# A gated cross-attention and quantised FFN layer: unrolled program, tiles batch by batch, int8 quantisation by conversion, 80 columns a head

## The reference

```
n  = layernorm(x)
q, k, v = n @ Wq, ctx @ Wk, ctx @ Wv            # per head 64 columns, 77 keys
x  = x + tanh(g_xattn) * (softmax(q k' / 8) v @ Wo + bo)
fq(t, f) = clip(round(t * 2**f), -128, 127) / 2**f
h  = relu(fq(fq(layernorm(x), 4) @ fq(w1, 6)' + fq(b1, 6), 4))    # 1024 hidden
x  = x + tanh(g_ffn) * (fq(h, 4) @ fq(w2, 6)' + fq(b2, 6))
```

## Time and profile before

| | |
|---|---|
| median of 3 executions | 143.04 us (142.93 to 143.25) |
| profiled execution: span | 141.0 us (no other time is given for it) |
| busy: PE / weight load | 133.5 us (95%) / 115.7 us (82%) |
| busy: DVE / ACT / POOL | 114.3 (81%) / 86.4 (61%) / 71.7 us (51%) |
| chain that ended last | PE 72%, DVE 14%, DMA 4%, issue 3%, ACT 3% |
| granted TensorE clock | 1.000 of full speed throughout |
| HBM read | 6.46 MB, nearly all in the first 21 us |

### The profile page before, as it was taken

One profiled execution on the slowest core, in us unless ns is written; L12 is line 12 of the kernel. 1 busy time (PEld: TensorE's weight loads), 2 busy tenths in 40 slices (PEclk: granted clock), 3 DMA queues, 4 the chain that ended last, 5 costly groups with the idle time before them and its releaser, 6 DMA issues.

```text
span 141.0 us, 3229 instructions
## 1 busy us (share of the span) xinstructions
PE 133.5 (95%) x1010; PEld 115.7 (82%) x1010; DVE 114.3 (81%) x282; ACT 86.4 (61%) x174; POOL 71.7 (51%) x104
## 2 busy tenths in 40 slices
PE   5959899999999999999999999999999999999991
PEld 2749898779998997989888898989898989768670
DVE  1077788998899999988987898889888889977572
ACT  3238174355877475894949495767757593828350
POOL 7522869989652753544555455544636364240200
PEclk9999999999999999999999999999999999999999
DMA  4999980000000000000020010002000200020204
GB/s 100 308 315 375 378 340 19 0 0 2 7 0 0 0 7 0 0 0 0 5 74 2 0 65 10 0 0 74 0 0 0 74 0 0 5 74 0 74 5 149
DMA packets 6295, 8.69 MB, mean 62 GB/s; under 512 B 489, under 2 KB 4237, under 8 KB 6285
## 3 DMA queue, kind: packets, MB, share of 16 engines
q1 hardware_dynamic: 6285, 8.56, 18.1%
HBM read 6.46 MB, written 2.10 MB: 61 GB/s over the span
## 4 chain that ended last, share of the span: by engine, by line
PE 72%; DVE 14%; DMA 4%; issue 3%; ACT 3%; POOL 1%; SPq 1%; DVEq 0%; ACTq 0%; POOLq 0%
PE sc_ps L840 17%; PE of_ps L912 16%; PE of_ps L953 7%; PE h_ps L944 6%; PE tr_ps L889 6%; DMA x_sb<-in_x_dram 4%; PE tr_ps L798 3%; PE tr_ps L868 2%; PE h_ps L868 2%; PE sc_ps L953 2%; PE of_ps L957 2%; DVE hid L659 2%; DVE den L594 2%; DVE mx L559 2%; PE tr_ps L777 1%
## 5 line engine op out<-in xcount | busy, mean ns | idle before, releaser
L912 PE MATMUL of_ps<-u_sb,pT 128*128 128x256 f32 x240 | 33.5, 288 | 0.0
L307 POOL TENSOR_TENSOR probs<-probs,rden 128x616 f32<-128x616 f32 x16 | 19.5, 1219 | 24.5 <-DVE rden L597 24.5
L840 PE MATMUL sc_ps<-a_sb,xT 128*128 128x308 f32 x192 | 31.3, 312 | 0.6 <-DVE a_sb L588 0.5
L912 PEld LDWEIGHTS of_ps<-u_sb,pT 128*128 128x128 f32 x240 | 29.7, 189 | 1.2 <-ACT pT L460 1.0
L840 PEld LDWEIGHTS sc_ps<-a_sb,xT 128*128 128x128 f32 x192 | 27.5, 188 | 1.4 <-DVE a_sb L588 0.7
L460 ACT CAST pT<-tr_ps 128x640 fp32r<-128x640 f32 x16 | 11.1, 692 | 23.2 <-PE tr_ps L889 23.2
L484 ACT ACTIVATE hid<-h_ps,b1z 128x256 f32 (+1 forms) x56 | 22.0, 480 | 0.5 <-PE h_ps L944 0.5
L314 POOL TENSOR_TENSOR rstd<-ve,mhalf 128x1 f32<-128x1 f32 x16 | 8.8, 553 | 21.4 <-DVE nm L631 21.4
L322 POOL TENSOR_TENSOR pT<-pT_full,pT 128x640 fp32r<-128x640 f32 x9 | 14.1, 1562 | 1.6 <-ACT pT_full L465 1.6
L944 PE MATMUL h_ps<-x2T,w1T 128*128 (+1 forms) x112 | 14.5, 273 | 0.0
L953 PE MATMUL of_ps<-w2T,hid 128*128 128x256 bf16 x104 | 13.6, 272 | 0.3 <-issue 0.3
(11 more groups left out here) (143 smaller groups left out, 221.4 us busy)
## 6 DMA issues: line engine op xcount, KB each, us to landing
x_sb<-in_x_dram SPq DMA_DIRECT2D x8, 256.0 KB, 7.2
w_sb<-in_L_ffn_w_dram SPq DMA_DIRECT2D x2, 1024.0 KB, 9.4
out_dram<-x_sb SPq DMA_DIRECT2D x7, 256.0 KB, 2.1
wk_sb<-in_L_xattn_Wk_dram SPq DMA_DIRECT2D x1, 512.0 KB, 3.8
wq_sb<-in_L_xattn_Wq_dram SPq DMA_DIRECT2D x1, 512.0 KB, 6.3
wv_sb<-in_L_xattn_Wv_dram SPq DMA_DIRECT2D x1, 512.0 KB, 9.8
wo_sb<-in_L_xattn_Wo_dram SPq DMA_DIRECT2D x1, 512.0 KB, 10.6
out_dram<-x_sb SPq DMA_DIRECT2D x2, 128.0 KB, 2.0
```

Of the source, the lines that this page charges most:

```text
L307: nc.gpsimd.tensor_tensor(v, v, rden[:, i, :].unsqueeze(2).to_broadcast([P, H, M]), ALU.mult).then_inc(probs_ready, 1)
L840: ins = nc.tensor.matmul(sc_ps[:, a, 0:HALF], xT[:, i, p, c, :], a_sb[:, q, c, i, HALF * a:HALF * a + HALF], start=first, stop=last)
L912: ins = nc.tensor.matmul(attn_ps, pT[:, i, p, P * c:P * c + P], u_sb[:, q, MC * i + c, :], start=first, stop=last)
```

## The change

The program is written anew with the same engines and the same arithmetic:

- **Order of tiles**: T = 8b + t, batch 0 first. Only batch 0's folded weights and U are made before slot 0; batch 1's are made in slots 0 to 3 (`score_weights(1, c)`, `output_weights(1, n)`), like w1's and w2's transposes. All slots are written out; there is no loop. x is looked ahead by 3 to 4 slots, scores by 2, hidden lags by 4, the second layer by 6.
- **80 columns a head**: probabilities have a pitch of 80 (3 padding columns). A chunk of U is then made of pieces of 32, 64 or 128 output rows at fixed places, ten a batch (`U_PIECES`), each one plain matmul with `tile_position`; bo is a matmul over 128 rows.
- **int8 by conversion**: writing to an int8 tile rounds and clamps. The second normalisation is one POOL instruction from x to int8; the hidden layer is a Relu on ACT to int8 (`hid_q`), widened to bf16 by POOL (`hidden_widen`, two copies of 512 columns); weights are rounded by ACT in one pass. Two int8 values are transposed as one bf16.
- **Engines**: the first normalisation moves from ACT to POOL; epsilon and the negated mean of the second from DVE to POOL; the low part of the probabilities is on POOL for tiles 0 to 3, on DVE for 4 to 15. Zeroing of kz and vz moves from POOL to DVE.
- **Second bias**: one bf16 row in a 128-row tile (`first_row`, `b2_row`), no offset, no DMA between tiles.
- **DMAs**: x comes in four pieces in the order of the batches, the first after wq; g comes broadcast to all rows.

The core of the diff:

```diff
-EARLY, LATE = 5, TILES - 2
+EARLY = 4
+U_PIECES = ((0, 0, 128, 0, 0),
+            (1, 0, 32, 0, 128), (1, 32, 32, 1, 0), (1, 64, 64, 1, 32),
+            (2, 0, 64, 1, 96), (2, 64, 64, 2, 0),
+            (3, 0, 64, 2, 64), (3, 64, 32, 2, 128), (3, 96, 32, 3, 0),
+            (4, 0, 128, 3, 32))
...
+            def output_weights(b, n):
+                for c, row, rows, j, col in U_PIECES:
+                    if c // 2 != n:
+                        continue
+                    dst = u_banks[b, n][:, D * (c % 2):D * (c % 2) + D]
+                    ins = nc.tensor.matmul(dst[row:row + rows, :], vz[:, b, j, col:col + rows], wo_sb[:, j, :],
+                                           start=True, stop=(c > 0), tile_position=(0, row))
+                    if c == 0:
+                        ins = nc.tensor.matmul(dst, bo_at[:, :], bo_pad[:, :], start=False, stop=True)
+                ins.then_inc(u_psum, 1)
...
+            # POOL
+            def normalise_first(T):
+                pool.wait_ge(rstd1_ready, T // 2 + 1)
+                if T >= 2:
+                    pool.wait_ge(xT_psum, T - 1)
+                nc.gpsimd.tensor_scalar(xn[:, T % 2, :], x_sb[:, T, :], rstd1[:, T:T + 1], nb1[:, T:T + 1],
+                                        ALU.mult, ALU.add).then_inc(xn_ready, 1)
+            def normalise_second(T):
+                i = T % 2
+                pool.wait_ge(mv2_ready, T + 1)
+                nc.gpsimd.tensor_scalar(ve2[:, i, :], mv2[:, i, 1:2], EPS, 1.0 / (AQ * AQ), ALU.add, ALU.mult).then_inc(ve2_ready, 1)
+                pool.wait_ge(ve2_ready, T + 1)
+                nc.gpsimd.tensor_tensor(rstd2[:, i, :], ve2[:, i, :], mhalf[:, 0:1], ALU.pow).then_inc(rstd2_ready, 1)
+                pool.wait_ge(rstd2_ready, T + 1)
+                nc.gpsimd.tensor_scalar(nb2[:, i, :], mv2[:, i, 0:1], rstd2[:, i, 0:1], -1.0, ALU.mult, ALU.mult).then_inc(nb2_ready, 1)
+                pool.wait_ge(nb2_ready, T + 1)
+                if T >= 2:
+                    pool.wait_ge(yT_psum, T - 1)
+                nc.gpsimd.tensor_scalar(yq[:, i, :], x_sb[:, T, :], rstd2[:, i, 0:1], nb2[:, i, 0:1],
+                                        ALU.mult, ALU.add).then_inc(yq_ready, 1)
+            def hidden_widen(k):
+                p, half = k // 2, k % 2
+                for n in range(2):
+                    if k == FC * 2 - 1 and n == 1:
+                        pool.wait_ge(hid_last, 1)
+                    else:
+                        pool.wait_ge(hid_rounded, 2 * k + n + 1)
+                    c = 4 * half + 2 * n
+                    nc.gpsimd.tensor_copy(hid[:, p, c:c + 2, :, :].rearrange("p c i r -> p (c i r)"),
+                                          hid_q[:, (2 * k + n) % 4, :]).then_inc(hid_ready, 1)
...
+            for s in range(TILES + 4):
+                if live(s - 1):
+                    normalise_second(s - 1)
+                if s == 0:
+                    rstd_first(3)
+                if s == 1:
+                    rstd_first(4)
+                if s < EARLY:
+                    probsT_low(s)
+                if live(s + 1):
+                    softmax_scale(s + 1)
+                if s == 2:
+                    hidden_bias()
+                    output_bias()
+                if s in (3, 4, 5):
+                    rstd_first(s + 2)
+                if 0 <= s - 4:
+                    hidden_widen(s - 4)
+                if live(s + 4):
+                    normalise_first(s + 4)
...
+            # ACT, hidden layer
+                for c in range(2):
+                    chunk = 4 * half + 2 * n + c
+                    ins = nc.scalar.activation(hid_q[:, (2 * k + n) % 4, D * c:D * c + D], h_ps[:, n, D * c:D * c + D],
+                                               ACT.Relu, bias=b1z[:, chunk:chunk + 1])
...
+            # DVE, one slot
+                if live(s - 1):
+                    residual(s - 1)
+                    stats_second(s - 1)
+                if live(s + 1):
+                    denominators(s + 1)
+                if s == 0:
+                    stats_first(3)
+                if s == 1:
+                    stats_first(4)
+                if s in (3, 4, 5):
+                    stats_first(s + 2)
+                if s >= EARLY:
+                    probsT_low(s)
+                if live(s + 3):
+                    rowsT_low(s + 3)
...
+                if live(s - 6):
+                    result(s - 6)
+                if live(s + 2):
+                    center(s + 2)
...
+            # PE, one slot
+            for s in range(TILES):
+                if live(s + 3):
+                    rowsT(s + 3)
+                if s == 0:
+                    pe.wait_ge(u_ready, 2)
+                    score_weights(1, 0)
+                probsT(s)
+                if s == 1:
+                    pe.wait_ge(a_ready, 3)
+                    score_weights(1, 1)
+                    weights1T()
+                if s == 2:
+                    pe.wait_ge(a_ready, 4)
+                    output_weights(1, 0)
+                    output_weights(1, 1)
+                if s == 3:
+                    pe.wait_ge(u_ready, 4)
+                    output_weights(1, 2)
+                    weights2T()
+                if s >= 4:
+                    hidden(s - 4)
+                if s >= 2:
+                    quantisedT(s - 2)
+                if s >= 6:
+                    ffn_out(s - 6)
+                if live(s + 2):
+                    scores(s + 2)
+                attend(s)
```

More of the change, by code:

```diff
@@ L11 @@
 F32R = mybir.dt.float32r
+I8 = mybir.dt.int8
 P = 128
@@ L148, in flamingo_kernel @@
[L148 to L159, removed]
+        attn_ps = of_ps[:, 0, 0:D]
@@ new lines, in rowsT_second, with round_weights @@
+            def rowsT_second(T):
+                act.wait_ge(yT_psum, T + 1)
+                nc.scalar.copy(x2T[:, T // 2, :, T % 2, :],
+                               yT_of(T).bitcast(I8).rearrange("p (r c) -> p c r", c=DK)).then_inc(x2T_ready, 1)
+            def round_weights(w_in, w_sb, w_q, done):
+                act.wait_ge(w_in, 16)
+                src, dst = w_sb[:, :, :].rearrange("p a b -> p (a b)"), w_q[:, :, :].rearrange("p a b -> p (a b)")
+                for h in range(2):
+                    nc.scalar.activation(dst[:, 1024 * h:1024 * h + 1024], src[:, 1024 * h:1024 * h + 1024], ACT.Copy,
+                                         scale=WQ).then_inc(done, 1)
@@ L517, in _ @@
[L517 to L529 removed]
+            a_copy(0, 0)
@@ new lines, in _ @@
+            residual(TILES - 1)
+            stats_second(TILES - 1)
+            for T in range(TILES - 6, TILES - 2):
+                result(T)
+            last = FC - 1
+            dve.wait_ge(hid_psum, 4 * TP)
+            dve.wait_ge(hid_ready, 4 * TP - 4)
+            for c in range(2):
+                chunk = FC - 2 + c
+                ins = nc.vector.tensor_scalar(hid_q[:, 3, D * c:D * c + D], h_ps[:, 1, D * c:D * c + D],
+                                              b1z[:, chunk:chunk + 1], 0.0, ALU.add, ALU.max)
@@ L749, in _ @@
+            ins.then_inc(hid_last, 1)
+            for T in range(TILES - 2, TILES):
+                result(T)
         @block.tensor
@@ new lines, in scores @@
+            def scores(T):
+                pe.wait_ge(xT_high, T + 1)
+                if T >= 1:
+                    pe.wait_ge(centered, T)
+                if T == TB:
+                    pe.wait_ge(a_ready, 2 * DK)
+                for p, q in PARTS:
+                    if p == 1:
+                        pe.wait_ge(xT_ready, T + 1)
+                    for c in range(DK):
+                        for a in range(2):
+                            first, last = (c, p, q) == (0, *PARTS[0]), (c, p, q) == (DK - 1, *PARTS[-1])
+                            ins = nc.tensor.matmul(sc_ps[:, a, 0:HALF], xT[:, T % 2, p, c, :],
+                                                   a_sb[:, q, T // TB, c, HALF * a:HALF * a + HALF], start=first, stop=last)
+                ins.then_inc(scores_ready, 1)
@@ new lines, in ffn_half, with ffn_bias, ffn_out @@
+            def ffn_half(T, half):
+                p, i = T // 2, T % 2
+                pe.wait_ge(hid_ready, 4 * p + 2 * half + 2)
+                for c in range(4 * half, 4 * half + 4):
+                    nc.tensor.matmul(ffn_of(T), hid[:, p, c, i, :], w2T[:, c, :], start=(c == 0), stop=False)
+            def ffn_bias(T):
+                nc.tensor.matmul(ffn_of(T), first_row[:, :], b2_row[:, :], start=False, stop=True).then_inc(ffn_psum, 1)
+            def ffn_out(T):
+                if T == 0:
+                    pe.wait_ge(w2T_ready, 2)
+                    pe.wait_ge(b2_ready, 1)
+                    pe.wait_ge(consts, 6)
+                elif T not in ffn_last:
+                    pe.wait_ge(result_ready, T)
+                ffn_half(T, 0)
+                ffn_half(T, 1)
+                ffn_bias(T)
```

1098 lines of the change are left out of this document (437 added, 661 removed).

## The result

The changed kernel takes 144.59 us (median of 4 executions, 144.03 to 145.75) against 143.10 for the one before: a ratio of 1.0101, 95% interval 1.0052 to 1.0151. It is slower, where 141.7 and faster were forecast. In what follows medians are over all executions of a kernel, while ratios leave out those more than 1.5% above its fastest. The profiled execution took 145.03 with a span of 143.1, so what lies around the span is 1.93 (2.04 was taken).

The account below looks back on a forecast made before the run. PE was taken to set the steady slots (6.7 to 6.2 us) and POOL the first six; slot 6 at 67.8, last attention at 125.8 and a 13.9 tail gave span 139.7, plus 2.04 made 141.7 us, range 137.6 to 147.

Parts of the forecast that it names:

- Steady slot: Repeating per-tile slot on PE: falls from 6.7 us to 6.2, range up to 6.5.
- The rival that the gaps stay: Steady slots: 0.2 us gaps stay without the loop, slots stay at 6.5 us, 143.7 us in all; chance 0.15.
- Slots 0 to 5: Early slots with batch 1's weights inside, scheduled from POOL's order: slot 0 at 23.1 us, slot 6 at 67.8.
- idle PE: Early slots: POOL costs the start about 6 us of PE standing idle.
- POOL's terms: POOL's work in a slot: 1.33 us to the statistics plus 4.5, 5.8 in all, against 6.2 on PE.
- the two-input price: Dearer end for POOL's new 256- and 512-column instructions: 1.98 ns a column, where one-input L344's price was taken.
- the slack: Steady slot: POOL's 5.8 us chain leaves 0.4 us against PE's 6.2.
- the second rival: POOL sets every slot: its chain 1.0 us longer, 7.2 us added, 148.9 us in all; chance 0.18.
- batch 1's output weights: Slot 2 on PE: ten matmuls taken at 4.7 us.
- the third rival: Output weight pieces overlap, start better than scheduled: 1.8 us less for each batch, 138.2 us in all; chance 0.22.
- Tail: After the last attention: 13.9 us with overlaps, against 12.2 before the change.
- The sign: Whole kernel: 141.7 us against a median of 143.04; faster 0.63, same 0.09, slower 0.28.

Follow-up runs that it names:

- the fill experiment: Changed kernel with ten more matmuls of 512 columns, result unused, inside attention(0) before its wait for the low part: 143.76 us, ratio 1.0044 against the kernel before.

## Why the prediction was wrong

The span is 3.4 us over the forecast. By stages, from the table above: slot 1 took 1.6 more than forecast, slot 3 1.1, slot 4 0.6, slot 5 0.1, the slots from 6 on 0.6 and the tail 0.6; slot 2 took 0.6 less, slot 0 0.2 less, and slot 0 began 0.4 early.

- **Steady slot, right.** 6.2 was worked out, 6.15 to 6.27 measured. The rival that the gaps stay (0.15) is ruled out. Only the last two slots are longer than forecast, by 0.6 together: attention takes 1.97 there where 1.77 was taken, and the last transposes of the probabilities 0.73.
- **Slots 0 to 5, the failed step.** The forecast had the waits in their places: attention(0) behind rstd_first(3), POOL at the end of slots 3, 4 and 5. It had their price wrong, in two ways.
- **First, idle PE was taken as time lost and nothing more.** For slot 1 the forecast said 32.3 to 39.1, 6.8 us; measured 8.36. The idle 2.4 us in slot 0 were followed by the halved clock, and the fill experiment, which keeps the clock at 1.00, gives back 1.1 of the 1.6. With the full clock slot 1 still takes 7.2 (31.78 to 38.97), and POOL ends it. No slice of the trace before had a clock below full, nor PE idle for long after the start, so the rows didn't offer the price. But the forecast itself listed idle PE and didn't ask what it costs: it said about 6 us, and its own entries for slots 0 to 5 (2.7 and 1.1, 1.0, 1.8, 0.6, 1.2) add up to 8.4.
- **Second, POOL's terms were too small.** 4.5 us after the statistics was taken; in slot 6 it runs from 70.09 to 74.93, 4.84. The two normalisations cost 0.16 more each than L344, which is nearly all of it. The forecast had named the two-input price as the other end (1.98 ns a column, 507 for 256 columns); 560 is above that, and below L322's 2.44 a column, while the widening came out at the price taken. In the slots with rstd_first, that took 1.6 where 1.4 was taken. Together this is the 0.6 of slot 4. In slot 3 a slip in the sum is added: 1.33, 1.7, 1.56, 1.22, 1.4 and 0.4 after attention(2) make 7.6, and not the 7.2 from 48.2 to 55.4. The steady chain too adds up to 5.9, where 5.8 was written, so the slack was 0.3 and not 0.4, and with the larger terms POOL touched PE in every second slot. By the forecast's own formula for the second rival, with an excess of 0.3 a slot, this is some 1 us on the time.
- **What the forecast didn't see is that a wait at the end of POOL's list is a choice of order.** It counted POOL's sum a slot and took the order as given. The same work in another order is worth 3.4 us (rstd_first) and some 4 (the place of the first normalisation).
- **Slots 2 and 3.** Not seen: the x2T copy stands behind 2 us of weight work on ACT (1.0 us in slot 2 and 1.4 in slot 3, the latter mostly hidden by POOL). The forecast had priced ACT by its sum, 4 us a slot, and not by its order in the slots with weight work. Against it, batch 1's output weights were cheaper than taken:

```profile
40.83 0.43 PE h_ps L664 x2
41.27 0.43 PE h_ps L667 x2
41.70 2.15 PE h_ps L664 x16
```

Ten matmuls in 3.0 us, 0.30 each, where 4.7 was taken, gaps of 0.33 to 0.41 in the weight loads at changes of width included. Batch 0's took 3.6 (16.5 to 20.1) where 5.2 was taken, but slot 0 began only 0.4 early: the first scores stood at 14.7 and not 14.2, and PE waited 0.5 for xn. The premise of the third rival, 1.8 less for each batch, was right, and its time was not: without this luck of 3.3 us in the weights the forecast would have missed by more. The Trainium skill, TensorEngine Tiling (Array Packing), Key Properties, has both rules, that a change of mode drains and that tiles run in parallel. The gaps at the changes of width agree with the first; that the eight partial pieces take 0.27 us each where the full ones take 0.43 agrees with the second, though no run here shows that pieces overlap.
- **Tail, 0.6 more.** 13.9 taken, 14.5 measured: DVE's last Relu stands behind result(13), which the forecast had no term for. With the order changed the trace has 13.3.
- **The sign.** The forecast margin, 1.3 us, was smaller than the sum of what it left out. No single cause makes up the 2.9 us between forecast and result: with the filler alone the kernel is still slower than before (143.76). The rival on the other side was put at POOL in every slot and priced at 148.9; what came was the milder form, POOL in the first six slots, with the clock on top. It should have been given more than 0.18, since POOL already bounded five slots in the forecast's own schedule and any error there counts at full.

## What to carry to other kernels

Where one engine is the bound and another feeds it once a slot, write down the place of the feeding instruction in its engine's list, not only the sum of the list: here the same work moved from the end of POOL's slot to its head was worth some 4 us (4.7 by the medians, 3.8 in the traces), and statistics needed two slots later, moved behind what PE waits for, 3.4. Price a pause of TensorE above its length: one of 2.4 us was followed by 6.8 us at half clock in some executions, and a repair that merged two short waits into a long one lost what it had gained. Then repair the orders together: one alone often only hands the wait on.

## What was not expected of the hardware

- After 2.4 us without work for PE the granted clock was 0.50 for 6.8 us in some executions, and 1.00 in others with the same pause (means of 0.974 to 1.0 over the changed kernel and the one with the first normalisation on ACT). Within one execution pauses of 2.4 and 2.27 us were followed by a fall and one of 2.46 was not. Ten unused matmuls in the pause kept it at or near 1.00.
- A POOL instruction on 256 columns with scale and bias per partition takes 560 ns, one on a single partition with immediates 403; writing int8 or float32 makes no difference, and int8 to bf16 over 512 columns takes 615.
- fp32 matmuls into pieces of 32 and 64 output rows take some 0.13 a pass in a run against 0.21 for full ones, and each change of width 0.33 to 0.41 of idle weight load.
